# Graph attention on one core: shorter last pieces, two quads of sums a slot near the end, a quad's tiles summed in one PSUM bank

## What is computed

```python
q, k, v, skip = x @ Wq + bq, x @ Wk + bk, x @ Wv + bv, x @ Ws + bs
logits = sum(q[dst] * k[src], axis=-1) / sqrt(128)
m = segment_max(logits, dst)
e = exp(logits - m[dst])
alpha = e / max(segment_sum(e, dst)[dst], 1e-16)
out = segment_sum(alpha[:, None] * v[src], dst) + skip      # relu between layers
```

## Time and profile before

| | |
|---|---|
| median of three runs | 7273.4 us (7272.12 to 7278.56) |
| span of the profiled execution | 7258.5 us |
| TensorE busy | 5523.8 us, 76% |
| VectorE busy | 4794.6 us, 66% |
| ScalarE busy | 2129.8 us, 29% |
| GpSimd busy | 4967.8 us, 68% |
| mean granted TensorE clock | 0.852 |

### The profile page before, as it was taken

How to read it: one execution, slowest core, us unless ns; L and a number is a source line. 1 busy time by engine, 2 the same in 40 slices (tenths; PEclk the granted TensorE clock), 3 DMA queues, 4 the chain that set the end, 5 groups by cost and what they waited for, 6 DMA issues and landing times. The chain is left out here.

```text
span 7258.5 us, 119802 instructions
## 1 busy us (share of the span) xinstructions
PE 5523.8 (76%) x30113; PEld 4158.0 (57%) x30113; DVE 4794.6 (66%) x20894; ACT 2129.8 (29%) x5508; POOL 4967.8 (68%) x5173
## 2 busy tenths in 40 slices
PE   4576577677777777777777767789898996898887
PEld 4433344466666556666556656566665665676665
DVE  7986578466666556666646666664545556888887
ACT  1044443211111411111411111343333333544454
POOL 5777774677777477777477777647475673777774
PEclk7687888788888878888878888899999998989898
DMA  9433352577777467777567777667566662222222
GB/s 307 131 84 82 77 116 49 171 209 207 209 209 207 145 197 206 211 207 210 162 178 209 207 205 208 180 176 210 160 206 187 201 206 82 56 56 56 56 57 54
DMA packets 911600, 1151.24 MB, mean 159 GB/s; under 512 B 143137, under 2 KB 676193, under 8 KB 911009
## 3 DMA queue, kind: packets, MB, share of 16 engines
q1 hardware_dynamic: 689200, 673.54, 30.8%
q0 software_dynamic: 202464, 461.07, 23.7%
q10 hardware_dynamic: 19346, 9.66, 0.5%
HBM read 882.09 MB, written 261.74 MB: 158 GB/s over the span
## 5 line engine op out<-in xcount | busy, mean ns | idle before, releaser
L487 POOL DMA_INDIRECT G<-table_kv,idx x2496 | 2382.7, 955 | 937.6 <-issue 744.7
L1591 DVE SCALAR_TENSOR_TENSOR sums<-ramp,place,bank 128x128 f32<-128x128 f32 x2496 | 717.9, 342 | 1195.8 <-PE bank L1538 1071.6
L1529 PE MATMUL bank<-ident,G 128*128 128x128 f32 x2496 | 659.8, 339 | 734.1 <-DMA G<-table_kv,idx 726.0
L1976 POOL DMA_INDIRECT G<-table_h,src_idx x864 | 823.9, 954 | 482.5 <-issue 258.4
L1510 ACT COPY slab<-bank 128x512 f32<-128x512 f32 x624 | 365.3, 585 | 2492.6 <-PE bank L1529 2489.4
L487 POOL DMA_INDIRECT G<-table_h,idx x832 | 829.8, 997 | 298.1 <-issue 228.8
L1538 PE MATMUL bank<-qT,slab 128*128 x4992 | 914.3, 340 | 104.3 <-issue 87.6
L1529 PEld LDWEIGHTS bank<-ident,G 128*128 128x128 f32 x2496 | 388.5, 165 | 959.0 <-DMA G<-table_kv,idx 913.4
L1538 PEld LDWEIGHTS bank<-qT,slab 128*128 128x128 f32 x4992 | 801.8, 244 | 205.0 <-issue 204.5
L534 PE MATMUL bank<-OH,sums 128*128 128x128 f32 x4992 | 852.1, 326 | 70.6 <-DVE sums L523 39.8
L534 PEld LDWEIGHTS bank<-OH,sums 128*128 128x128 f32 x4992 | 767.1, 235 | 105.0 <-DVE OH L514 87.9
(11 more groups left out here) (342 smaller groups left out, 8750.1 us busy)
## 6 DMA issues: line engine op xcount, KB each, us to landing
stash<-G SPq DMA_DIRECT2D x312, 512.0 KB
sums<-stash SPq DMA_DIRECT2D x624, 256.0 KB
sums<-adjacency SPq DMA_DIRECT2D x294, 522.5 KB
adjacency<-same SPq DMA_DIRECT2D x49, 1184.0 KB
same<-adjacency SPq DMA_DIRECT2D x90, 522.5 KB
G<-table_kv,idx POOLq DMA_INDIRECT x2496
sums<-adjacency SPq DMA_DIRECT2D x48, 408.0 KB
table_kv<-G SPq DMA_DIRECT2D x72, 256.0 KB, 3.1
```

What stands on the lines that cost most here:

```text
L487: pool.indirect_dma_start(G[:, s, 0:width], None, tab, bass.IndirectOffsetOnAxis(ap=idx[:, s:s + 1], axis=0)).then_inc(c_gather[s].sem, 16)
L1529: ins = pe.transpose(bank[q % 2][:, (s % QUAD) * P:(s % QUAD + 1) * P], G[:, s, 0:D], ident[:])
L1591: ins = dve.scalar_tensor_tensor(scratch[:, s % QUAD, :], ramp[:], place[:, bass.ds(t * SLOTS + s, 1)], bank[2 + q % 2][:, (s % QUAD) * P: ...
L1976: pool.indirect_dma_start(G[:, s, 0:D], None, table[l], bass.IndirectOffsetOnAxis(ap=src_idx[:, DENSE + t:DENSE + t + 1], axis=0)).then_in ...
```

## The change

The 52 turns are cut into twelve pieces of four, one of three and one of one. From slot 180 on a slot may sum two quads, where their weights are there; the softmax of pieces 11 and 12 (the two before the very last) takes two stages a slot. For the quads from 152 on, TensorE first writes zeros over a whole bank with one matmul of bf16 zeros, then adds the four tiles into it, each at its place in the quad (a register per tile), and DVE adds the bank to `aggT` with one instruction of 512 columns. One-hots: up to quad 151 all four by DVE; 152 to 191 two by DVE and two by ACT; 192 to 203 two by ACT and two by POOL; 204 to 207 DVE one, ACT two, POOL one. SP's stores and loads are written out by slot. The order of edges is loaded by nine DMAs, not three. The functions that aren't shown are rewritten from turns and pieces to slots without another change in what they do; the links are the same, over 48 and 16 tiles in the last two pieces.

```diff
 PIECE_TURNS = 4
-PIECES = TURNS // PIECE_TURNS
+WHOLE_PIECES = 12
+PIECE_LENGTHS = (PIECE_TURNS,) * WHOLE_PIECES + (3, 1)
+PIECES = len(PIECE_LENGTHS)
+PIECE_AT = [sum(PIECE_LENGTHS[:c]) for c in range(PIECES)]
 PT = PIECE_TURNS * SLOTS
 LAG = PIECE_TURNS + 3
+LAG_QUADS = LAG * QUADS
+ALL_QUADS = TURNS * QUADS
+HASTE = 180
+LATE = HASTE - LAG_QUADS
+LATE_QUADS = ALL_QUADS - LATE
...
+        zero = sb("zero", [P, 2 * P])
+        quad_at = sb("quad_at", [P, LATE_QUADS], I32)
+        tile_in_quad = sb("tile_in_quad", [P, LATE_QUADS * QUAD], I32)
...
+        def dve_quad_places(then, settled):
+
+            late_start = start[:, LATE * QUAD:].rearrange("p (q k) -> p q k", k=QUAD)
+            then(dve.tensor_scalar(quad_at[:], late_start[:, :, 0], float(NW - QUAD * P), None, ALU.min))
+            settled()
+            then(dve.tensor_tensor(tile_in_quad[:].rearrange("p (q k) -> p q k", k=QUAD), late_start,
+                                   quad_at[:].unsqueeze(2).to_broadcast([P, LATE_QUADS, QUAD]), ALU.subtract))
+            dve.memset(zero[:], 0.0)
+
...
                 for k in range(3):
-                    sp.dma_start(order[k].rearrange("t (c p) -> t c p", p=P), a["dst_line"][k:k + EP].rearrange("(c t p) -> t c p", t=PT, p=P)).then_inc(order_in.sem, 16)
+                    whole_edges = WHOLE_PIECES * PT * P
+                    sp.dma_start(order[k][:, 0:WHOLE_PIECES * P].rearrange("t (c p) -> t c p", p=P),
+                                 a["dst_line"][k:k + whole_edges].rearrange("(c t p) -> t c p", t=PT, p=P)).then_inc(order_in.sem, 16)
+                    for c in range(WHOLE_PIECES, PIECES):
+                        first, n = PIECE_AT[c] * SLOTS * P, PIECE_LENGTHS[c] * SLOTS
+                        sp.dma_start(order[k][0:n, c * P:(c + 1) * P], a["dst_line"][k + first:k + first + n * P].rearrange("(t p) -> t p", p=P)).then_inc(order_in.sem, 16)
...
+        def stage_slot(c, k):
+
+            return end_quad(c) + (k // 2 if HASTY_PIECE <= c < PIECES - 1 else k)
+
+        def weights_slot(c):
+            return stage_slot(c, STAGES - 1) + 1
+
+        def sums_by_slot():
+
+            found, q, n = {}, 0, LAG_QUADS
+            while q < ALL_QUADS:
+                most = 1 if n < HASTE else 2
+                found[n] = []
+                while len(found[n]) < most and q < ALL_QUADS and weights_slot(piece_of(q)) <= n and n != ALL_QUADS:
+                    found[n].append(q)
+                    q += 1
+                n += 1
+            return found
+
+        SUMS = sums_by_slot()
+        SUM_SLOT = {q: n for n, quads in SUMS.items() for q in quads}
+        ALL_SLOTS = max(SUMS) + 1
+        RESCALED = {c: weights_slot(c) if c >= HASTY_PIECE else SUM_SLOT[first_quad(c)] for c in range(PIECES)}
+        DRAIN = min(q for q in range(ALL_QUADS) if SUM_SLOT[q] >= ALL_QUADS)
+        LAST = first_quad(PIECES - 1)
...
+        def onehot_ahead(q):
+
+            return q + 2 if q + 2 < ALL_QUADS and (q + 2 - first_quad(piece_of(q + 2)) >= 2 or piece_of(q + 2) < HASTY_PIECE) else None
+
+        def first_onehots(n):
+
+            return [first_quad(c) + k for c in (0, *range(HASTY_PIECE, PIECES)) if (weights_slot(c) if c else LAG_QUADS) == n for k in range(2)]
+
+        def dve_makes(q):
+            return range(QUAD) if q < LATE else (0, 3) if q < DRAIN else () if q < LAST else (3,)
+
+        def pool_makes(q):
+            return () if q < DRAIN else (0, 3) if q < LAST else (0,)
...
+            stores = [(QUADS * t + 2 * h + 1, 0, t, h) for t in range(EVEN_TURNS + LAG - 1, TURNS) for h in range(2)]
+            loads = [(SUM_SLOT[q - QUADS], 1, q // QUADS, q % QUADS) for q in range(EVEN_TURNS * QUADS, ALL_QUADS)]
+            for _, is_load, t, part in sorted(stores + loads):
+                if is_load:
+                    load(t, part)
+                else:
+                    store(t, part)
...
+                for x in first_onehots(n) + [onehot_ahead(x) for x in SUMS.get(n, ())]:
+                    if x is not None and x >= LATE:
+                        act_late_onehots(x)
...
+            def sums_of(q):
+                t, part = divmod(q, QUADS)
+                into = bank[SUM_BANKS[q % 2]]
+                if q >= LATE:
+                    n = (q - LATE) * QUAD
+                    _, places = nc.values_load_multi_w_load_instructions(
+                        tile_in_quad[0:1, n:n + QUAD], engines=(PE,), min_val=0, max_val=(QUAD - 1) * P,
+                        skip_runtime_bounds_check_because="a tile holds P nodes at most, and each node has an edge")
+                pe.wait_ge(c_added.sem, c_added.at((q - 1) * QUAD))
+                if q >= LATE:
+                    pe.matmul(into[:, :], zero_by_zero[:, 0:P], zero_by_zero[:, :], start=True, stop=False)
+                if dve_makes(q):
+                    pe.wait_ge(c_onehot.sem, c_onehot.at(dve_quads(q + 1)))
+                if q >= LATE:
+                    pe.wait_ge(c_late_act.sem, c_late_act.at(q + 1 - LATE))
+                if pool_makes(q):
+                    pe.wait_ge(c_late_pool.sem, c_late_pool.at(pool_onehots(q + 1)))
+                quad_loaded(t, part * QUAD)
+                for k in range(QUAD):
+                    s = part * QUAD + k
+                    if q < LATE:
+                        ins = pe.matmul(into[:, k * P:(k + 1) * P], v_rows[:, s, :], OH[:, s, :], start=True, stop=True)
+                    else:
+                        ins = pe.matmul(into[:, bass.ds(places[k], P)], v_rows[:, s, :], OH[:, s, :], start=False, stop=k == QUAD - 1)
+                ins.then_inc(c_rows.sem, 1)
...
+                if n < ALL_QUADS:
+                    turn(n)
+                for c, k in stages_in(n - 2)[1:]:
+                    if k in HOP_OF_STAGE:
+                        hop(c, HOP_OF_STAGE[k])
+                if 0 < n <= ALL_QUADS:
+                    scores(n - 1)
+                for c, k in stages_in(n - 1)[:1]:
+                    if k in HOP_OF_STAGE:
+                        hop(c, HOP_OF_STAGE[k])
+                for q in SUMS.get(n, ()):
+                    sums_of(q)
...
+            def weigh_and_add(q_onehot, q_add, between):
+                late = q_add is not None and q_add >= LATE
+                if late:
+                    _, windows = nc.values_load_multi_w_load_instructions(
+                        quad_at[0:1, q_add - LATE:q_add - LATE + 1], engines=(DVE,), min_val=0, max_val=NW - QUAD * P,
+                        skip_runtime_bounds_check_because="starts are dst values, clamped to the last quad of blocks")
+                elif q_add is not None:
+                    windows = windows_of(DVE, q_add // QUADS, q_add % QUADS)
+                mine = dve_makes(q_onehot) if q_onehot is not None else ()
+                if mine:
+                    if q_onehot == first_quad(piece_of(q_onehot)):
+                        dve.wait_ge(c_link.sem, c_link.at(piece_of(q_onehot) * LINKS + WEIGHTS_LINK))
+                    dve.wait_ge(c_rows.sem, c_rows.at(q_onehot + 1 - QUADS))
+                for k in range(QUAD):
+                    if k in mine:
+                        s, t = slots_of(q_onehot)[k], q_onehot * QUAD + k
+                        ins = dve.tensor_scalar(OH[:, s, :], ramp[:], place[:, t:t + 1], weight[:, t:t + 1], ALU.is_equal, ALU.mult)
+                        if k == mine[-1]:
+                            ins.then_inc(c_onehot.sem, 1)
+                    between()
+                    if q_add is not None and not late:
+                        if k == 0:
+                            dve.wait_ge(c_rows.sem, c_rows.at(q_add + 1))
+                        w = aggT[:, bass.ds(windows[k], P)]
+                        dve.wait_ge(c_added.sem, c_added.at(q_add * QUAD + k))
+                        dve.tensor_tensor(w, w, bank[SUM_BANKS[q_add % 2]][:, k * P:(k + 1) * P], ALU.add).then_inc(c_added.sem, 1)
+                    elif late and k == QUAD - 1:
+                        dve.wait_ge(c_rows.sem, c_rows.at(q_add + 1))
+                        w = aggT[:, bass.ds(windows[0], QUAD * P)]
+                        dve.wait_ge(c_added.sem, c_added.at(q_add * QUAD))
+                        dve.tensor_tensor(w, w, bank[SUM_BANKS[q_add % 2]][:, :], ALU.add).then_inc(c_added.sem, QUAD)
+                    between()
+
+            links = [softmax(c) for c in range(PIECES)]
+            taken = [0] * PIECES
+
+            def take(c, to):
+                if taken[c] < to:
+                    taken[c] += 1
+                    next(links[c], None)
+
+            for n in range(ALL_SLOTS):
+                for c in range(PIECES):
+                    if RESCALED[c] == n:
+                        take(c, LINKS)
+                        dve.wait_ge(c_link.sem, c_link.at((c + 1) * LINKS))
+                if n < ALL_QUADS:
+                    pick(n)
+                stages = stages_in(n)
+                skip = [3]
+
+                def between():
```

(53 more changed lines are left out.)

247 lines of the change are left out of this document (128 added, 119 removed).

## The result

The changed kernel takes **7344.5 us** (median of 4 runs, 7339.3 to 7349.8), the kernel before 7272.8 (4 runs, 7271.3 to 7278.6). The ratio is **1.0103**, 95% interval 1.0089 to 1.0117: slower by 72 us. The forecast was 7376, range 7265 to 7425, slower with 0.80.

What follows compares the result with a forecast made beforehand. POOL's gather issue was taken to bound the gather phase, with a drain behind it. Loss 51 less gain 17 is 34 us a layer, 102 for three, plus 1 set-up and 14.9 from span to median: 7376 us, range 7265 to 7425.

Steps and rivals of the forecast that it cites:

- POOL paces the phase, and one can only lose there: Gather phase of each attention layer: POOL's issue of 1.25 us a gather sets 5.0 us a slot; nothing to win.
- The loop: Two-quad slots: scores, pick, one-hots, add, two sums, transposes, scores wait in a circle; TensorE is held 2.32 us.
- The double slot, 7.8 us: A gather-phase slot summing two quads: 7.32 us at TensorE's full level, taken as 7.8, ends 6.8 and 8.6.
- The low level: TensorE at 1.2 GHz in double slots: 3.1 to 3.7 us more when low, weighted to 0.5 to 1.2.
- Slots with softmax, 3 us for all: Slots 180 to 182 also hold piece 10's last three softmax stages, partly in the loop: 3 us a layer.
- Loss in the phase, 51 us a layer (30 to 65): Gather phase: twenty double slots at 7.8 instead of 5.03 cost 55 us, less 7 hidden, plus 3 for softmax.
- Gain in the drain, 17 (10 to 24): After the last transposes: 66 us a layer falls to 49, with 9 slots and 16 quads instead of 28 each.
- Set-up 1 us (0 to 3): Before the first table: six more DMAs for the order of edges and three small DVE instructions cost 1 us.
- Span to median, 14.9: Whole kernel: the median of runs lies 14.9 us over the profiled span, a difference kept for the forecast.
- Hidden loop: Rival: double slots fit under the gathers, faster at 7223 us if a slot is under 6.1 us; chance 13%.
- Low level throughout: Rival: TensorE's low clock holds through all double slots, 9.5 us a slot, 207 us more, 7480; chance 7%.
- Transfers: Rival: a double slot's DMA takes 6.5 us at 202 GB/s, 4.5 at full share; adds nothing; no chance given.

Runs made afterwards that it cites:

- four-add kernel: The changed kernel without zeroing matmul and wide add: four sums side by side and four adds a quad; 7465.3 us, ratio to before 1.0270.
- last kernel: The changed kernel with adds before the pick, softmax links behind the adds from slot 180, and piece 11's sums starting one slot later; 7228.6 us, ratio to before 0.9939.
- one-bank kernel: The kernel before with only the one-bank accumulation, zeroing and wide add for the last 26 quads, one quad a slot; 7235.7 us, ratio 0.9956.
- first experiment: The changed kernel with DVE making a slot's one-hots and adds before its pick of logits from slot 180 on; 7275.6 us, ratio to before 1.0012.
- links-behind-adds kernel: The changed kernel with adds before the pick and, from slot 180, softmax links behind them; 7240.5 us, ratio to before 0.9958; in the slow set 9600.3 us, 0.9994.

## Why the prediction was right, point by point

- **POOL paces the phase, and one can only lose there**: right. With one quad a slot the phase is 135.5 to 139 us, and no kernel with the usual transfers was below 135.5.
- **The loop**: right in its links and its DVE half (2.32 predicted, 2.37 measured). It is shown by the three runs that put work into it, put the same work beside it, and took it apart by order.
- **The double slot, 7.8 us**: too long. At full level it takes 6.18 (scores at 2281.45 to scores at 2287.63), against my 7.32. The step that failed is adding up durations of rows and an idle time for every register load. From start to start it is zeroing 0.23, sums 0.99, zeroing 0.21, sums 0.89, transposes 0.44, where I had 0.3, 1.06, 0.25 + 0.3, 1.06, 0.60 + 0.28. No idle time stands where I had put a register load. Over the nine slots 183 to 191 (from the end of one turn to that of another) the mean is (2315.46 - 2252.90) / 9 = 6.95 us; the first of them, with the end of a softmax, took 8.41, and the eight quiet ones 6.77 (6.92 and 6.93 in the other layers). So the low level costs 0.6 to 0.8 where I took 0.5.
- **The low level**: the granted clock of the phase is 0.81 with TensorE busy 64% of the time. The rule of the Trainium skill that I weighed (TensorE: Matmul & The Clock Gate, Part 1), as I read it, would have had the slots at full level; the trace speaks against that for this kernel, and for the four-add kernel more so: 0.73 at a busy 63%, with the longer wait in each slot. Against this stands 0.92 at 62% in the quiet drain of before, where the pauses are 0.7 us; and where the loop is gone, in the double slots of the last kernel, it is 1.00 at a busy 81%, as the rule would have it. Which property of the pauses decides isn't settled by these runs.
- **Slots with softmax, 3 us for all**: too small. Slots 180 to 183 took 7.5, 9.2, 10.1 and 8.4 us, 8 us over four quiet ones, and the slot in which piece 11 begins took 11.5, another 4.7. I had named the first and not seen the second: the weights are ready in the slot that wants the one-hots made from them.
- **Loss in the phase, 51 us a layer (30 to 65)**: 41.4. In the first layer twenty slots at the quiet rate, 1.75 over 5.03, would make 35, where I had 55; the slots with softmax and the start of piece 11 add 13, where I had 3; 44 was measured, so the empty slots and POOL's lead gave back about 4, where I took 7. Two terms that were too favourable hid most of the one that was too dear, 13 of 20 us: that much of the agreement is luck.
- **Gain in the drain, 17 (10 to 24)**: 17.6. The three parts partly make up for each other. To the first sum 11.3 us (2406.42 to 2417.70) for 10.0, the six slots 26.5 for 29, the end 10 for 9 and 1. ACT's quad is 1.59 and not 1.75, the granted clock 0.74 and not 0.87. The terms of my drain slot add up to 5.3, not 5.2.
- **Set-up 1 us (0 to 3)**: the start of the first gather moved by 4.4, but by -4.5 in the one-bank kernel and +0.2 in the first experiment, which has the same set-up; it is within the scatter.
- **Span to median, 14.9**: wrong as a name. What lies around a span is 1.8; the rest was how the one execution stood to its median. I let it stand as a constant, and that is why 84 of span came out as 72 in the medians. Of the 31 us by which the forecast was too high, 18 are of the sum and 13 of this.
- **The rivals.** *Hidden loop*, decided at 6.1 us: the slot was 6.15 at the very best and 6.95 in the mean, nearer to that point than I had thought, so 13% was fair or low; with the adds ahead of the pick it comes true for the quiet slots. *Low level throughout*: no, 0.81. *Transfers*: not the bound, with 179 GB/s in the phase against 202 before, and with shorter slots at up to 258 GB/s where only the order and one start were changed.

In sum: 51 - 17 became 41.4 - 17.6, 24 us a layer instead of 34. The mechanism stood; the term that was mis-sized is the double slot, 6.8 us in the quiet ones instead of 7.8.

## What to carry to other kernels

When a stage of a software pipeline takes two items a slot instead of one, look-ahead counted in items halves in slots, and an order that no one waited for turns into a loop between two engines: walk that loop from start to start, and put the work that others wait for ahead of what itself waits. Price the parts of a change one by one: here a gain of 32 us was buried under a loss of 109, and with the order mended the costlier part still isn't shown to add to the 32. And test "is this engine the bound" by adding the same work once inside and once outside of the suspected path.

## What was unexpected of the hardware

- **The rate of the transfers differed between sets of runs.** The same kernel before took 7268 to 7273 us in four sets and 9612 in one. In the middle of its first gather stretch the links-behind-adds kernel moved 143 GB/s there, at a DMA share of 0.49, lower than 0.70 and 202 GB/s in the earlier trace rows, with a granted clock of 0.69 and POOL waiting for the stash:

```profile
1900.00:3100.00 1200.00, 645.02 (x3401) 555.19 (x3402) 518.32 (x2768) 127.24 (x399) 641.75 (x675) 0.69 0.49 143
```

```profile
POOL G L498 <- DMA stash<-G: 211.5, 31, 10.9
```

  Why is open. Kernels can be compared within a set, or between sets in which the kernel before took the same time.
- **Zeroing a bank of 512 columns with bf16 zeros is cheap**: 0.38 to 0.39 us by its record, 0.21 to 0.23 from its start to that of the next matmul at full level.
- **The wide add is as dear as two and a half narrow ones**, 0.684 us against four at 1.55 in a row, and with it the waits of one add for another are gone.
